# An involution with softmaxed taps on one Trainium2 core: 32x32 array tiles, untransposed accumulation, two taps per product

## What is computed

```python
x1 = conv1x1(x, w1, b1)                       # 32 channels
x2 = conv1x1(x, w2, b2)                       # 32 channels
x3 = conv1x1(x, w3, b3)                       # 256 channels
sub2 = x1[:, :, None] - unfold_patches(x2)    # 49 taps, reflect padding
feat = concatenate([sub2, subp], axis=1)      # subp: 2 position channels
y = relu(bn_eval(feat, bn1...))
y = conv1x1(y, cw1)                           # 34 -> 32
y = relu(bn_eval(y, bn2...))
wgt = conv1x1(y, cw2, cb2)                    # 32 -> 32
wgt = softmax(wgt, axis=2)                    # over the 49 taps
for i in range(7):
    for j in range(7):
        out = out + patch(x3, i, j) * wgt[:, :, idx]   # 8 channels share a weight
```

## Time and profile before

| | |
|---|---|
| median of 3 runs | 4254.01 us (4253.61 to 4260.93) |
| span of the profiled execution | 4333.9 us |
| own time of the profiled execution | not listed apart from its span |
| PE (matmul) busy in the span | 3640.3 us, 84% |
| VectorE (DVE) | 2902.6 us, 67% |
| ScalarE (ACT) | 2306.3 us, 53% |
| GpSimd (POOL) | 1641.7 us, 38% |
| mean granted TensorE clock | 0.930 of 2.4 GHz |

### The profile page before, as it was taken

How to read it: one execution, slowest core, us unless ns; L and a number is a source line. 1 busy time by engine, 2 the same in 40 slices (tenths; PEclk the granted TensorE clock), 3 DMA queues, 4 the chain that set the end, 5 groups by cost and what they waited for, 6 DMA issues and landing times. The chain is left out here.

```text
span 4333.9 us, 64637 instructions
## 1 busy us (share of the span) xinstructions
PE 3640.3 (84%) x24130; PEld 2345.7 (54%) x24130; DVE 2902.6 (67%) x2667; ACT 2306.3 (53%) x3514; POOL 1641.7 (38%) x734
## 2 busy tenths in 40 slices
PE   5779899898889989997688978888988889288787
PEld 1257777777777777776334342434333342256565
DVE  6258888888888888887767574767566673643311
ACT  1376667666667766663354637454654645342221
POOL 1257877777877777886000000000000000224422
PEclk9899999999999999999799999999999999588898
DMA  5500101110101110101201110111112010424433
GB/s 198 157 32 31 40 17 41 40 36 31 41 20 38 41 36 32 40 12 58 57 1 53 43 41 12 51 52 24 23 56 57 1 24 30 140 89 146 136 114 116
DMA packets 119427, 238.94 MB, mean 55 GB/s; under 512 B 22246, under 2 KB 83982, under 8 KB 116018
## 3 DMA queue, kind: packets, MB, share of 16 engines
q1 hardware_dynamic: 107266, 203.22, 15.0%
q0 software_dynamic: 11392, 31.02, 2.2%
q10 hardware_dynamic: 432, 0.20, 0.0%
HBM read 135.85 MB, written 79.27 MB: 50 GB/s over the span
## 5 line engine op out<-in xcount | busy, mean ns | idle before, releaser
L712 DVE TENSOR_TENSOR prod<-ps,win 128x1792 f32<-128x1792 f32 x630 | 1241.4, 2018 | 159.9 <-PE ps L783 116.1
L783 PE MATMUL ps<-ident,prod 128*128 128x128 f32 x8820 | 1093.6, 280 | 168.3 <-DVE prod L712 152.9
L783 PEld LDWEIGHTS ps<-ident,prod 128*128 128x128 f32 x8820 | 1027.6, 145 | 313.0 <-DVE prod L712 170.1
L1699 POOL DMA_DIRECT2D ident<-in_ident x1 | 0.6, 578 | 1627.7 <-POOLq L925 1627.7
L1168 ACT ACTIVATE phq<-ps 128x896 f32<-128x896 f32 x448 | 384.7, 918 | 201.0 <-PE ps L1431 200.1
L1266 DVE TENSOR_TENSOR phk<-kv 128x2048 f32<-128x2048 f32 (+1 forms) x200 | 455.9, 2282 | 1.2 <-issue 0.7
L468 POOL TENSOR_TENSOR y<-a1w,x2w 128x1568 f32<-128x1568 f32 x98 | 320.8, 3274 | 326.6 <-PE ps L763 308.3
L611 ACT ACTIVATE ps<-lg 128x448 f32<-128x448 f32 (+1 forms) x322 | 315.2, 982 | 239.9 <-DVE prod L712 239.9
L632 ACT ACTIVATE lg<-ps,par 128x392 f32<-128x392 f32 x392 | 390.9, 997 | 32.7 <-PE ps L770 31.3
L625 ACT ACTIVATE y<-ps,u2c,s2c 128x392 f32<-128x392 f32 x392 | 266.8, 681 | 223.9 <-PE ps L763 221.8
L762 PE MATMUL ps<-y,cw1bd 128*128 128x392 f32 x784 | 330.2, 503 | 36.2 <-ACT y L618 29.0
(11 more groups left out here) (264 smaller groups left out, 5314.3 us busy)
## 6 DMA issues: line engine op xcount, KB each, us to landing
win<-planes SPq DMA_DIRECT2D x14, 2480.0 KB, 8.7
qst<-qsp SPq DMA_DIRECT2D x96, 196.0 KB, 4.5
planes<-stage SPq DMA_DIRECT2D x7, 1984.0 KB, 7.0
xs<-in_x SPq DMA_DIRECT2D x8, 1568.0 KB, 21.3
conv_dram<-osb SPq DMA_DIRECT2D x14, 896.0 KB, 4.6
t<-in_x SPq DMA_DIRECT2D x28, 448.0 KB, 4.0
xn<-conv_dram SPq DMA_DIRECT2D x28, 448.0 KB, 6.9
t_dram<-tout SPq DMA_DIRECT2D x28, 448.0 KB, 2.9
```

What stands on the lines that cost most here:

```text
L712: v.tensor_tensor(prod[b.buf(t)][:].rearrange("p (s h w) -> p s h w", h=RW, w=W), w, xw, ALU.mult).then_inc(prod_ready, 1)
L783: mm = pe.matmul(acc[:, at:at + P], x[:, at:at + P], ident[:], start=(t == 0 and k % 4 == 0), stop=(t == NU - 1), is_transpose=True, skip_ ...
```

## The change

- PE works in 32x32 tiles of its array. The stationary operand of a tap's addition is a 32x32 block of the identity and the product is the moving operand, so nothing is transposed. A product now lies as (row, channel, column) in a partition. Tile (`r`, `h`) moves image `r`, row `h` to partitions 32 `h` of bank 4 + `r`: 16 matmuls of 448 columns per tap. The accumulator comes out with (row, weight channel) in the partitions and needs no turning: `turn` and `give` are gone, and `take` writes straight to `osb`.
- The denominators are summed by PE too, from `lg`, in 56 further columns of the same banks: 16 short matmuls for each of the 49 taps (`total`). GpSimd's sums and `dsum` are gone.
- GpSimd multiplies nine taps instead of four (`own`) and adds none; PE adds each from two buffers in turn.
- VectorE multiplies two taps per instruction (`pair`): 20 instructions of 3584 elements.
- The chain goes in 14 chunks of two image rows (half of a tap row), over the 32x32 diagonal blocks of `cw1` and `cw2`, 8 + 8 + 8 matmuls each; ScalarE's `second` and `third` handle 784 elements from two banks. `y2` has one buffer, so a chunk's `first` waits until the chunk before has its logits. `lg` is laid out as (row, tap, column) and is written and read without the stride of seven.
- PE's waits are made by its sequencer for all tiles (`await_ge`). The store is four DMAs, the position features come in four DMAs per tap row, and the involution's result in DRAM has channels ahead of images.

```diff
@@ -319,32 +319,25 @@
-NPROD = 3
-OWN = 4
+OWN = 9
 ND = TAPS - OWN
-OWN_TAPS = (0,) + tuple(range(ND + 1, TAPS))
-NU = ND + 1
-CPI = RW
-NCH = K7 * CPI
+NPAIR_D = (ND + 1) // 2
+NCH = 2 * K7
 CW = K7 * W
-SUMC = SHARE * PW
-NBACK = (SUMC + 511) // 512
-HALF = 1024
-GAP = 8
...
+HC = SHARE * W
+SUMC = RW * HC
+DENC = HC + W
+CH_AT = [1 + c for c in range(NCH)]
+MAX_AT = [CH_AT[2 * i + 1] + 2 for i in range(K7)]
+FOLD_AT = MAX_AT[-1]
+EXP_NOW = {FOLD_AT + 1: 0, FOLD_AT + 2: 1}
+EXP_NEXT = {1: (2,), 2: (3,), 3: (4,), 4: (5,), 5: (6,)}
+FIRST_AT = [0] + [2 * i for i in range(1, K7)]
+POOL_ORDER = [("z", 0), ("shift", 2), ("z", 1), ("shift", 3), ("shift", 4), ("z", 2), ("shift", 5), ("shift", 6), ("z", 3),
+              ("own", 0), ("z", 4), ("own", 1), ("z", 5), ("own", 2), ("z", 6)] + [("own", k) for k in range(3, OWN - 1)]
+OWN_AT = [7, 9, 11, 13, 14, 15, 16, 17, 19]
+DEN_A_TICK = 3
...
+            def own(b, k):
+                t = ND + k
+                i, j = t // K7, t % K7
...
+                if k == 0 and not b.early(1):
+                    pool.wait_ge(acc_done, b.n)
+                if k == 1 and not b.early(1):
+                    pool.wait_ge(stored, 16 * RW * b.n)
+                if k >= 2:
+                    pool.wait_ge(own_used, (OWN - 1) * b.n + k - 1)
...
+                for kind, k in POOL_ORDER:
+                    if a and kind == "z":
+                        z(a, k)
+                    if b and kind == "shift":
+                        shift(b, k)
+                    if b and kind == "own":
+                        own(b, k)
...
-                sp.dma_start(conv_v[:, :, bass.ds(m * PW, PW)],
-                             osb[:, 0:SUMC].rearrange("p (s x) -> p s x", x=PW)).then_inc(stored, 16)
+                for h in range(RW):
+                    sp.dma_start(conv_v[:, :, bass.ds(m * PW + h * W, W)],
+                                 osb[32 * h:32 * h + 32, 0:SHARE].rearrange("p s b w -> p (s b) w")).then_inc(stored, 16)
...
+                act.wait_ge(acc_done, m + 1)
+                if not (isinstance(m, int) and m < 1):
+                    act.wait_ge(stored, 16 * RW * m)
+                act.activation(osb[:, :, 2 * k:2 * k + 2].rearrange("p s b w -> p b s w"),
+                               ps[:, 4 + 2 * k:6 + 2 * k, 0:DENC].rearrange("p b (s w) -> p b s w", w=W), ACT.Copy).then_inc(acc_out, 1)
...
+                    act.wait_ge(prod_ready, NPAIR_D * b.n + p - 1)
...
-                    if not (a.early(1) and c < 2):
-                        act.wait_ge(mm2, g - 1)
-                    act.activation(y2[c % 2][:], y2p, ACT.Relu, scale=s2c[:], bias=u2c[:]).then_inc(relu2, 1)
+                    act.activation(y2[:], ps[:, 0:2, 0:CW], ACT.Relu, scale=s2c[:], bias=u2c[:]).then_inc(relu2, 1)
...
+                def pair(p):
+                    n = min(2, ND - 2 * p)
...
-                    w = wps[:, (t // 2 + b.par) % 2, PW * (t % 2):PW * (t % 2) + PW].rearrange("p (h w) -> p h w", w=W).unsqueeze(1).broadcast_to([P, SHARE, RW, W])
-                    xw = win[b.par][:, i:i + RW, 0:SHARE, j:j + W].rearrange("p h s w -> p s h w")
-                    v.tensor_tensor(prod[b.buf(t)][:].rearrange("p (s h w) -> p s h w", h=RW, w=W), w, xw,
-                                    ALU.mult).then_inc(prod_ready, 1)
...
+                    v.wait_ge(w_out, NPAIR_D * b.n + p + 1)
+                    if not (b.early(1) and p < 2):
+                        v.wait_ge(summed, NPAIR_D * b.n + p - 1)
+                    w = ps[:, 2 + p % 2, 0:n * PW].rearrange("p (n h w) -> p n h w", h=RW, w=W).unsqueeze(3).broadcast_to([P, n, RW, SHARE, W])
+                    at = [t // K7 * SHARE * WP + t % K7 for t in range(2 * p, 2 * p + n)]
+                    x = win[b.par][:]
+                    xw = bass.AP(x.tensor, x.offset + at[0], [x.ap[0], [at[-1] - at[0], n], [SHARE * WP, RW], [WP, SHARE], [1, W]])
+                    o = prod[p % 2][:, 0:n].rearrange("p n (h s w) -> p n h s w", s=SHARE, w=W)
+                    v.tensor_tensor(o, w, xw, ALU.mult).then_inc(prod_ready, 1)
...
+            def await_ge(s, n):
+
+                pe.wait_ge(s, n)
+                pe.sem_inc(passed, 1)
...
+                        await_ge(logit, a.g(c))
+                    y, f = y1[a.qpar(i)], pf[a.qpar(i)]
+                    for q in range(2):
+                        for r in range(B):
+                            h, at = 2 * hh + q, 64 * q + 32 * (r % 2)
+                            pe.matmul(ps[at:at + 32, r // 2, 0:CW].rearrange("p (j w) -> p j w", w=W), diag(cw1, r),
+                                      y[32 * r:32 * r + 32, :, h * W:(h + 1) * W], start=True, stop=False)
...
+                def add(x, begin, end):
+                    for h in range(RW):
+                        for r in range(B):
+                            if begin and h == 0 and r % 2 == 0 and not b.early(1):
+                                await_ge(acc_out, 2 * b.n - 1 + r // 2)
+                            mm = pe.matmul(ps[32 * h:32 * h + 32, 4 + r, 0:HC], diag(ident, r), x[32 * r:32 * r + 32, h * HC:(h + 1) * HC],
+                                           start=begin, stop=end, skip_group_check=True)
+                    return mm
...
+                        mm.then_inc(acc_done, 1)
+
+                def total(t):
+                    i, j = t // K7, t % K7
+                    if j == 0:
+                        await_ge(exped, b.q(i) + 1)
+                    for h in range(RW):
+                        for r in range(B):
+                            mm = pe.matmul(ps[32 * h:32 * h + 32, 4 + r, HC:DENC], diag(ident, r), lg[b.par][32 * r:32 * r + 32, i, h, j, :],
+                                           start=False, stop=(t == TAPS - 1), skip_group_check=True)
+                    return mm
...
+                        pair(u, 0)
+                    if a and u in CH_AT:
+                        second(CH_AT.index(u))
+                    if b:
+                        if 2 * u + 1 < ND:
+                            pair(u, 1)
+                        for t in range(DEN_A_TICK * (u - 1), min(DEN_A_TICK * u, TAPS)):
+                            if t >= 0:
+                                total(t)
+                        for k in range(OWN):
+                            if OWN_AT[k] == u:
+                                own(k)
```

More of the change, by code:

```diff
@@ L486, in total @@
[L486 to L496, removed]
@@ L510, in taps @@
[L510 to L535 removed]
+                m = mx[:].rearrange("p (h w) -> p h w", w=W).unsqueeze(2).broadcast_to([P, RW, K7, W])
@@ L663, in slot @@
                     take(b.n, 1)
-                    for p in range(NBACK):
-                        give(b.n, p)
             act.dma_start(cw1[:], cw1_bd).then_inc(w_in, 16)
@@ L717, in slot @@
                         rowmax(MAX_AT.index(u))
+                    if a and u == FOLD_AT:
+                        fold()
                     if b and not b.early(1) and u == RECIP_AT:
@@ L721, in slot @@
                         scale(b.n - 1)
-                    if a and u == FOLD_AT:
-                        fold()
-                    if b and u < ND:
-                        unit(u)
+                    if b:
+                        pair(u)
                 if not a:
@@ L787, in slot @@
-                for u in range(NU):
-                    if a and u in CH_AT:
-                        c = CH_AT.index(u)
-                        first(c)
-                        if c >= 1:
-                            second(c - 1)
-                    if a and u == LAST_LOGIT:
-                        second(NCH - 1)
-                    if b:
-                        unit(u)
-                    if b and not b.early(1) and u in BACK_AT:
-                        turn(b.n - 1, BACK_AT.index(u), a)
@@ new lines, in pair, with own @@
+                def pair(p, k):
+                    if k == 0:
+                        await_ge(prod_ready, NPAIR_D * b.n + p + 1)
+                    mm = add(prod[p % 2][:, k], p == 0 and k == 0, False)
+                    if 2 * p + k == min(2 * p + 1, ND - 1):
+                        mm.then_inc(summed, 1)
+                def own(k):
+                    await_ge(own_ready, OWN * b.n + k + 1)
+                    mm = add(own_buf[k % 2], False, k == OWN - 1)
+                    if k < OWN - 1:
+                        mm.then_inc(own_used, 1)
+                    else:
+                        mm.then_inc(acc_done, 1)
@@ new lines, in slot @@
+                for u in range(NPAIR_D):
+                    if a and u in CH_AT:
+                        first(CH_AT.index(u))
+                    if b:
+                        pair(u, 0)
+                    if a and u in CH_AT:
+                        second(CH_AT.index(u))
+                    if b:
+                        if 2 * u + 1 < ND:
[6 more added lines that the diff above has]
+                                own(k)
```

277 lines of the change are left out of this document (81 added, 196 removed).

## The result

The changed kernel takes 4276.7 us (4259.2 to 4284.8, 4 runs) against 4255.4 for the kernel before in the same comparison: ratio 1.0042, 95% interval 1.0026 to 1.0058. It is 0.4% slower, where 3900 was forecast.

A forecast was written before the change was run, and what follows sets the result against it. PE was taken to set the slot's pace, VectorE close behind; slots of 103 instead of 128.7 us save 334, prologue 7, last slot 15: 356 us, scaled to 349, giving 3900; range 3800 to 4190.

The forecast's parts named there:

- PE, the term in dispute: PE's steady slot: taps 36.8, denominators 17.2 and chain 20.6 us, sum 75 us against 117, if all 16 tiles overlap.
- the prologue: Before the first row maximum: 14 serial chunks of 4.1 us plus 12, taken as 70 us where 77 were, less 7.
- the last slot: Last block to its store: 112 us becomes 20 x 3.87 + 10 to start + 9 to close, about 97, less 15.
- Rival 3: Weight loads or instruction fetching set the pace: 42 ns a pair, 155 us for 3696 pairs, about 4590 us; chance 0.11.
- rival 1: Tile row groups serialise by half: a tap costs 1.49 us, PE's slot 120 us, time about 4220; chance 0.10.
- Rival 2: Pairs go out slower than tiles take them: 25 ns a pair, slot 121 us, time about 4150; chance 0.11.
- VectorE, mis-sized: VectorE's steady slot: pairs 77.4, maxima 12.5, fold 1.8, reciprocal 1.55, scaling 2.0; sum 95.2 us, 14 less than before.
- The scaling laid at 2.0: VectorE's scaling after the reciprocal in each slot, expected to cost like one old product, 2.0 us.
- GpSimd 81 for 88.2: GpSimd's slot: z 22.9, shifts 20.7 and nine own products 44.6, sum 88.2 us against 100.5.
- ScalarE 58 for 62: ScalarE's slot with half as many, larger evictions and fewer weight copies: 62 us against 86.5.
- The chain's round of 5.2 us: One serial chunk round with its adds on PE and ScalarE: 5.2 us; 14 such ticks and 6 at 3.9 give 96 us.
- The scaling by 0.98: Profiled span 4333.9 us was 80 above the runs' median, so the 356 us saving was scaled by 4254 / 4334.

The follow-up runs named there:

- 5232 pairs: Changed kernel with a second add of 8 columns after each denominator add except the last tap's: 4889.8 us, ratio 1.1495, slot 168.9 us.
- the block's last part: Changed kernel plus constant adds over 16 tiles before the first chunk: 1536 records each of 448, 56, 8 columns (46.0, 43.1, 43.5 us), lastly 768 of 448.
- the flat maximum: Changed kernel with row maxima and fold reading 7 memory neighbours: 4272.4 us, ratio 1.0037; the same plus row sums on GpSimd: 4105.5 us, ratio 0.9451.

## Why the prediction was wrong

- **Failed step: "PE, the term in dispute", "at that pace the 32 of one denominator tap take 0.35 us at most".** The 11 ns came from 8 records inside one burst. Over many packets a pair takes 28 ns, so the sum isn't 75 us but at least 103.5. The other 22 us of the slot are a remainder, taken here as TensorE's waits for products and relus; they stay 22 with 5232 pairs. Of the 377 us between 3900 and 4277 the slots are 13 x (125.8 - 103) = 296, the prologue 30 and the last slot 33. Rival 3 named the mechanism and the 0.5 MB a slot (measured 0.51), but priced it by 42 ns in another place and gave it 0.11; its point of decision, 35 ns a pair, lies beside the 34.0 measured in the slot (125.8 / 3696).
- **Right: 16 tiles overlap.** The records of 448 columns take 28.6 ns each at full clock where one tile alone holds one for 373, 13 times the pace, and that is the supply's. Where the clock was 0.50 and the supply no bound (the block's last part, from 316.9 us), 128 records took 5.9 us, 46 ns each, against 2 x 373: 16 times. So rival 1 is out.
- **A misread figure.** The 10.6 times of the Trainium skill ("TensorE: Matmul & The Clock Gate", part 3) would put a tap at 32 x 373 / 10.6 = 1.13 us by an estimate, not near 0.75. These runs show more overlap than that.
- **Rival 2's 25 ns.** The same page of the Trainium skill ("Back-to-back issue gap") has it as the floor from one matmul to the next. It isn't the floor of a burst (11 ns), but comes near the sustained 28. Rival 2's slot of 121 us is 5 short; its 4150 also kept the gains of the prologue and the last slot.
- **VectorE, mis-sized: 106 us for 95.2.** Pairs took 3.885 us (3.87). The stride "taken as free" costs 1.34 us a row, the fold 2.95 for 1.8: 10.5 us a slot, worth nothing at TensorE's pace, 0.9% once it is relieved. The scaling laid at 2.0 took up to 16.7, in turns with GpSimd.
- **GpSimd 81 for 88.2, ScalarE 58 for 62:** own products took 3.71 us in place of 4.95; shifts 3.66 in place of 2.97.
- **The chain's round of 5.2 us is 7.05** (starts of L569 from 714.2 to 742.4 in four rounds). That the adds in it are late by the supply fits, and wasn't tried apart.
- **Prologue: 7 us less became 23 more.** I had 5.6 us a chunk at 1.2 GHz as an aside and took 4.1; the granted clock was 0.50, with TensorE busy for 48.7 us of 100, and chunks took 5.8 and 7.2 us in turn (starts of L683 at 184.20, 189.99 and 197.18). The last slot, 15 less, became 18 more: its twenty products, laid at 77 us, take 107.6 (1923.4 to 2031.0). The 3136 pairs beside them need 88 at 28 ns; the rest isn't taken apart.
- **The scaling by 0.98 has no ground:** the 80 us by which the profiled execution before is longer lie behind the involution. It moves the sum by 7 us only.
- **Right:** nobody waits for the stores or the pf loads from 400 to 1913 us, and the granted clock of the twelve steady slots stayed at 0.96, as before.

## What to carry to other kernels

Count the instructions of an engine and not only its columns: before work is cut into small tiles, multiply pairs of load and matmul by the sustained 28 ns measured here and set that against the slot. A gap taken from a handful of records in a row is the price in a burst, not of a stream. And when one engine sets the pace, a saving on another is worth nothing until it is relieved, as the flat maximum shows (0 and 0.9%).
